# A four-layer graph network on one core: the third layer's factored rows stored a chunk later, the first layer's softmax weights by three VectorE operations and two exponents

## The reference, cut to what matters

```python
x = _layernorm(x + _L0_gnn_ref(x, edge_index, edge_weight, edge_attr_64, ...))
x = _layernorm(x + _L1_gnn_ref(x, src, dst, W1, b1, W2, b2))
x = _layernorm(x + _L2_gnn_ref(x, weight, src, dst, edge_type_8))
x = _layernorm(x + _L3_gnn_ref(x, W_e, b_e, W_n, b_n, src, dst, edge_type_3, node_type_3))

# first layer, per edge and head (alpha is the score)
alpha = jnp.where(alpha >= 0, alpha, 0.2 * alpha)
amax = jax.ops.segment_max(alpha, dst, num_segments=n)
ex = jnp.exp(alpha - amax[dst])
denom = jax.ops.segment_sum(ex, dst, num_segments=n)
attn = ex / (denom[dst] + 1e-16)
out = jax.ops.segment_sum(v[src] * attn[:, :, None], dst, num_segments=n)

# third layer
hw = jnp.einsum('ni,rio->nro', h, weight)     # 8 relations
out = jax.ops.segment_sum(hw[src, rel], dst, num_segments=n_nodes)
```

## Time and profile before

| | |
|---|---|
| median of 3 runs | 1840.75 us (1837.97 to 1842.14) |
| the profiled execution's own time | 1843.65 us |
| its span | 1841.9 us |
| busy: PE, DVE, ACT, POOL | 78%, 77%, 60%, 67% of the span |
| moved by DMA | 205.06 MB, 111 GB/s in the mean |
| mean granted TensorE clock | 0.89 of full speed |

### The profile page before, as it was taken

The page is one execution under the profiler, slowest core; times in us unless marked ns, Lnnn a source line. Parts: engine busy times, 40 slices in busy tenths (PEclk is TensorE's granted clock), DMA queues, the critical chain, the costliest instruction groups (busy, mean ns, idle before and its releaser), DMA issues.

```text
span 1841.9 us, 22899 instructions
## 1 busy us (share of the span) xinstructions
PE 1438.7 (78%) x6078; PEld 924.2 (50%) x6078; DVE 1419.5 (77%) x3056; ACT 1111.6 (60%) x2769; POOL 1237.0 (67%) x910
## 2 busy tenths in 40 slices
PE   4788888888886677777677767766677599999995
PEld 2555555555554566666544444443444355555553
DVE  5798999999998699999876565555665577887874
ACT  1687878787878588888854444444445434434432
POOL 7888887777788777788664444444454258888874
PEclk8788888888888799999898888888788899999998
DMA  6344444444434467676623333333333433433420
GB/s 161 96 101 109 108 106 104 109 105 112 108 94 117 103 164 184 186 186 187 177 75 93 92 92 93 110 104 107 96 82 86 131 88 93 103 92 93 107 77 21
DMA packets 165797, 205.06 MB, mean 111 GB/s; under 512 B 66825, under 2 KB 97920, under 8 KB 165668
## 3 DMA queue, kind: packets, MB, share of 16 engines
q1 hardware_dynamic: 108068, 179.45, 35.3%
q0 software_dynamic: 57600, 24.15, 7.7%
HBM read 147.12 MB, written 70.80 MB: 118 GB/s over the span
## 4 chain that ended last, share of the span: by engine, by line
PE 49%; DVE 19%; ACT 12%; issue 10%; DMA 6%; SPq 3%; POOL 0%; DVEq 0%; ACTq 0%; POOLq 0%
PE po L1369 21%; DMA rel<-in_etype 6%; PE pb L1604 6%; PE pt L1358 6%; DVE bst L755 5%; DVE run L830 3%; PE pc L1478 2%; ACT x L1067 2%; PE po L1364 2%; PE po L1429 2%; ACT so L1263 2%; DVE masked L965 2%; PE pa L1618 2%; PE pa L1645 1%; PE pb L1645 1%
## 5 line engine op out<-in xcount | busy, mean ns | idle before, releaser
L533 POOL DMA_INDIRECT xs<-target_rows,slot_all x236 | 320.6, 1359 | 290.9 <-DMA xs<-source_rows 213.9
L1067 ACT ACTIVATE x<-y,nmr,rst 125x128 f32<-125x128 f32 x800 | 322.5, 483 | 162.5 <-DVE nmr L780 161.7
L1369 PE MATMUL po<-wnt,rt 128*125 128x384 f32 x800 | 297.6, 518 | 0.0
L965 DVE SCALAR_TENSOR_TENSOR masked<-rel,st 128x500 f32<-128x500 int32 x175 | 107.0, 671 | 189.0 <-DMA rel<-in_etype 173.3
L1358 PE MATMUL pt<-ident,x 125*128 125x125 f32 x800 | 133.0, 293 | 112.4 <-issue 112.4
L1369 PEld LDWEIGHTS po<-wnt,rt 128*125 128x125 f32 x800 | 162.8, 206 | 97.3 <-issue 21.8
L1369 PE MATMUL po<-wnt,run 128*125 128x384 f32 x600 | 201.5, 486 | 0.0
L540 POOL DMA_INDIRECT out_rows<-do,last_all x100 | 146.5, 1465 | 65.4 <-issue 44.7
L1358 PEld LDWEIGHTS pt<-ident,x 125*128 125x128 f32 x800 | 102.4, 155 | 149.8 <-issue 148.8
L533 POOL DMA_INDIRECT xs<-in_x,src_all x100 | 146.0, 1460 | 34.6 <-issue 34.3
L1067 ACT ACTIVATE do<-yd,nmr,rst 125x128 f32<-125x128 f32 x400 | 163.7, 483 | 6.2 <-DVE nmr L780 6.2
(11 more groups left out here) (190 smaller groups left out, 3106.5 us busy)
## 6 DMA issues: line engine op xcount, KB each, us to landing
xin<-in_x SPq DMA_DIRECT2D x100, 224.0 KB
out_rows<-res SPq DMA_DIRECT2D x100, 224.0 KB
source_rows<-so SPq DMA_DIRECT2D x75, 224.0 KB
target_rows<-do SPq DMA_DIRECT2D x75, 224.0 KB
xs<-source_rows SPq DMA_DIRECT2D x59, 224.0 KB
same<-same_d SPq DMA_DIRECT2D x50, 250.0 KB
rel<-in_etype SPq DMA_DIRECT2D x50, 250.0 KB
xd<-target_rows SPq DMA_DIRECT2D x46, 224.0 KB
```

The lines of the kernel that those rows point to most:

```text
L533: return nc.gpsimd.indirect_dma_start(out=to, out_offset=None, in_=table, in_offset=bass.IndirectOffsetOnAxis(ap=index, axis=0), bounds_ch ...
L965: V.scalar_tensor_tensor(out=masked[:, r, :], in0=rel[b][:, :], scalar=float(r), in1=st[:, :], op0=ALU.is_equal, op1=ALU.mult).then_inc(q[ ...
L1067: last = A(to[:, j, :], y[:, j, :], ACT.Identity, scale=rst[s][:, k:k + 1], bias=nmr[s][:, k:k + 1])
L1369: last = mm(po[0:R, j * 512:j * 512 + NT * D], left(j), wnt[:, k, :, :].rearrange("k t d -> k (t d)"), start=start, stop=stop, skip_group_ ...
```

## The change

Two things change. In SP's loop of the third layer, `store_sources2(c + 1)` stands where `store_sources2(c + 2)` stood, and ahead of the loop `sources2(3)` is issued before `store_sources2(0)`, while `store_sources2(1)` moves into the loop. In the first layer, the scan adds `aux` first and takes the maximum with the score second, so that `run` holds the running maximum itself; `aux` is no longer shifted. VectorE then makes both exponents' arguments itself (three operations for one), and ScalarE takes two exponents, without the two Relus. A DMA of 4 bytes and a memset at the start fall away.

```diff
@@ SP @@
-            sp.dma_start(row(start_d[0:1, 0:E]), start_p[:, :]).then_inc(s_scr, 16)
-            sp.dma_start(start_d[0:1, E:E + 1], start_p[0:1, 0:1]).then_inc(s_scr, 16)
+            sp.dma_start(row(start_d), start_p[:, :]).then_inc(s_scr, 16)
...
-                sp.dma_start(aux[b][:, :], start_d[0:1, bass.ds(c * C + 1, C)].broadcast_to([D, C])).then_inc(q["aux"][b], 16)
+                sp.dma_start(aux[b][:, :], to_all(start_d, c)).then_inc(q["aux"][b], 16)
...
-            sp.wait_ge(s_scr, 32)
+            sp.wait_ge(s_scr, 16)
...
             stored(1)
+            sources2(3)
             store_sources2(0)
-            sources2(3)
-            store_sources2(1)
...
                 if c >= 1:
                     store2(c - 1)
-                if there(c + 2):
-                    store_sources2(c + 2)
+                if there(c + 1):
+                    store_sources2(c + 1)
                 store_dense(d - 7)
@@ VectorE @@
-            V.memset(run[:, 0, 0:1], -BIG)
...
-                step(scan(run, 0, score, aux[b][:, :], ALU.max, ALU.add))
-                V.tensor_tensor(wb, run[:, 0, 0:C], score, ALU.subtract).then_inc(q["vE"], 1)
+                step(scan(run, 0, aux[b][:, :], score, ALU.add, ALU.max))
+                step(V.tensor_tensor(wb, run[:, 0, 0:C], aux[b][:, :], ALU.add))
+                V.tensor_tensor(wa, score, run[:, 0, 1:C + 1], ALU.subtract)
+                V.tensor_tensor(wb, wb, run[:, 0, 1:C + 1], ALU.subtract).then_inc(q["vE"], 1)
@@ ScalarE @@
-            def differences0(c):
-                q = ph[0]
-                act.wait_ge(q["vE"], c + 1)
-                A(wa, wb, ACT.Relu)
-                A(wb, wb, ACT.Relu, scale=-1.0).then_inc(q["eR"], 1)
-
             def weights0(c):
                 q = ph[0]
-                act.wait_ge(q["eR"], c + 1)
-                A(wb, wb, ACT.Exp, scale=-1.0)
-                A(wa, wa, ACT.Exp, scale=-1.0).then_inc(q["eX"], 1)
+                act.wait_ge(q["vE"], c + 1)
+                A(wb, wb, ACT.Exp)
+                A(wa, wa, ACT.Exp).then_inc(q["eX"], 1)
...
                     evacuate_rt(2 * c)
-                    differences0(c + 1)
                     evacuate_xt(2 * c)
                     weights0(c + 1)
```

More of the change, by code:

```diff
@@ L68, in gnn_kernel @@
     same_d = nc.dram_tensor("same_d", [1, E], F32).ap()
-    start_d = nc.dram_tensor("start_d", [1, E + 1], F32).ap()
+    start_d = nc.dram_tensor("start_d", [1, E], F32).ap()
     rdeg_d = nc.dram_tensor("rdeg_d", [1, E], F32).ap()
@@ L173, in gnn_kernel @@
         SOONER = 13
-        SINGLE = ("tS tD eS eD eL pA pB pR vA vE vL eX eR nS nD nF yb eN sc", "tS tD eS eD pR vA nS nD rd vF",
+        SINGLE = ("tS tD eS eD eL pA pB pR vA vE vL eX nS nD nF yb eN sc", "tS tD eS eD pR vA nS nD rd vF",
                   "tS eS pM pR vA vM nD nF nS", "tS tD eS eD pM pR vM vA eX vN nD rd bs xb")
@@ L1144, in slopes0, with weights0 @@
                 A(score, pc[:, 0:C], ACT.Copy, scale=0.2).then_inc(q["eL"], 1)
-            def differences0(c):
+            def weights0(c):
                 q = ph[0]
                 act.wait_ge(q["vE"], c + 1)
-                A(wa, wb, ACT.Relu)
-                A(wb, wb, ACT.Relu, scale=-1.0).then_inc(q["eR"], 1)
-            def weights0(c):
-                q = ph[0]
-                act.wait_ge(q["eR"], c + 1)
-                A(wb, wb, ACT.Exp, scale=-1.0)
-                A(wa, wa, ACT.Exp, scale=-1.0).then_inc(q["eX"], 1)
+                A(wb, wb, ACT.Exp)
+                A(wa, wa, ACT.Exp).then_inc(q["eX"], 1)
             def sums0(c):
@@ L1178, in _ @@
             slopes0(0)
-            differences0(0)
             weights0(0)
```

## The result

The changed kernel takes 1774.55 us (median of 4 runs, 1769.67 to 1775.76) beside 1840.06 us for the kernel before: a ratio of 0.964, 95% interval [0.962, 0.966], 65.5 us less. The forecast was 1767, the range 1736 to 1796. The profiled executions give 69.0 us between their spans, 1841.9 and 1772.9.

What follows compares the result with a forecast made beforehand. The prediction took a ring of waits through the types' load to bound the third layer: 22 turns of 3.42 us (-75) and +2 for the first layer gave 1770.7 against the profiled 1843.65, so 1767 against the median, range 1736 to 1796.

Steps and rivals of the forecast that it cites:

- The bound and the ring: Third layer: bound by no engine but by a ring of waits through the types' load, one turn 22.39 us.
- Issue time, 2.57 us a turn: Third layer, SP's queue: 2.57 us a turn saved from the end of L1263 to the issue of rel.
- rel's own wait: Third layer: rel's wait for the masks of c+1 is met at 1207.8, over 7 us before L1263 ends.
- The landing, 0.85 us: Third layer: rel lands 4.2 us after issue with 250 KB ahead instead of 1 MB, a gain of 0.85.
- Rival (a): Third layer: only issue time is saved, rel still lands 5.07 us after it; 1786 us, chance 0.15.
- TensorE's part at nothing: Third layer: TensorE's pieces in the ring change with the clock, either sign possible; none taken in the sum.
- (c): Third layer: the clock holds, the ring's eight matmuls take 3.36 us instead of 5.43; 1721 us, chance 0.1.
- (d): Third layer: the slow stretch falls on the matmuls, 6.72 us instead of 5.43; 1795 us, chance 0.1.
- 22 turns alike: Third layer: 3.42 us saved in each of 22 turns, -75 us.
- (e): Third layer: rel comes a whole turn earlier and 173.3 us of waits go; 1669 us, chance 0.02.
- The first layer: First layer: VectorE's added 1.36 us a chunk eats idle time of 1.43; bounds 0 to 34 us, +2 taken.
- rival (f): First layer: slower, 1.36 us on top of each of 25 chunks, +34 us; 1875 with no third-layer gain; chance 0.03.

Runs made afterwards that it cites:

- types_first: The kernel after, with the types' load issued ahead of the sources' load and its wait for ScalarE's factored rows: 1664.54 us, ratio 0.905.
- types_once: The kernel after, with the types' load left out of the third layer's loop (first two chunks' types used for all): 1665.36 us.
- pair_between: The kernel after, with one pair of DMAs (the dense store) put back between the sources' load and the types' load: 1804.60 us, ratio 0.981.
- types_last: The kernel after, with the targets' and same flags' loads issued ahead of the wait for ScalarE's factored rows: 1742.80 us, ratio 0.947.
- weights_only: The kernel before with only the first layer's weights changed, the third layer as before: 1843.04 us, ratio 1.001.
- vector_more: The kernel after, with two more VectorE tensor_tensor of 128x500 in each chunk of the first layer: 1806.82 us, ratio 0.982 to the kernel before.

## Why the prediction was right or wrong, point by point

- **The bound and the ring: right.** The types' load closed the ring; types_first and types_once show that with this load early, or gone, no other ring holds a turn above the engines' own 13.1 us. The turn of 22.39 us that the prediction shows is one of the longer ones; the mean is 21.28.
- **The wait moves, it doesn't go: right.** SP's wait for L1263 moved to the sources' load.
- **Issue time, 2.57 us a turn: right in a full turn, 2.40 in the mean.** From the end of the factored rows to the issue of rel it is mostly 0.86 us for 3.39. In the last three of the 19 turns the kernel before had no dense load in front any more (2.56 us), so there was less to save.
- **rel's own wait: a misreading without effect.** The text before the prediction and the prediction let `relations2(c + 2)` wait for the masks of chunk c+1. The code (L382 of the kernel after) waits for those of chunk c, which used the same buffer and were done a turn earlier.
- **The landing, 0.85 us: mis-sized.** It is 0.30 (5.16 to 4.86, means of 21 and 19 turns). I counted the 750 KB that left the front, and not that the same 750 KB now follow without a stop, where SP stood before. pair_between moves one pair (250 KB) from behind to the front again and costs 0.24 us of landing; types_last takes two loads away from right behind and gains 1.0. Rival (a) had the right reason, that it shares the DMA engines with what follows, and lay nearer in this term. What the bytes in front cost with the same ones behind, no run shows.
- **TensorE's part at nothing: right here.** The engines' part is 12.91 us for 12.97, though the mean clock of 1000 to 1300 us rose from 0.81 to 0.87. Of the rivals on the clock neither came: the relation matmuls on masked copies took 618 ns in the mean for 628, where (c) wanted them at the full clock and (d) slower. (d)'s effect fits pair_between, 649 ns at a mean clock of 0.84, 0.48 us a turn; (c)'s begins in types_last, 599 ns, and is whole in types_first, 582 ns in the same window and a clock of 1.00 up to 1220 us. The groups of 1000 to 1300 us, of before, after, pair_between and types_last (busy us, mean ns):

```profile
L1604 PE MATMUL pb<-masked,wr 128*128 128x500 f32 x190 | 92.3, 628 | 0.0
```

```profile
L1595 PE MATMUL pb<-masked,wr 128*128 128x500 f32 x224 | 106.6, 618 | 0.0
```

```profile
L1597 PE MATMUL pb<-masked,wr 128*128 128x500 f32 x210 | 105.9, 649 | 0.0
```

```profile
L1595 PE MATMUL pb<-masked,wr 128*128 128x500 f32 x249 | 114.2, 599 | 0.0
```

The busy times of 1000 to 1300 us of the kernel before, the kernel after and types_last, with the clock third from the end:

```profile
1000.00:1300.00 300.00, 206.58 (x717) 125.32 (x716) 178.13 (x386) 132.35 (x341) 134.75 (x98) 0.81 0.35 98
```

```profile
1000.00:1300.00 300.00, 238.14 (x832) 144.48 (x832) 207.46 (x454) 156.48 (x402) 157.04 (x113) 0.87 0.40 114
```

```profile
1000.00:1300.00 300.00, 252.94 (x905) 152.79 (x904) 225.08 (x489) 169.76 (x436) 171.36 (x122) 0.90 0.43 118
```

- **22 turns alike: wrong.** 19 turns gave 2.76 us each, and the last two 12.1 us together. I had read the wait of sources2 as always in front of relations2, and gave (e) 0.02; the code's `if there(c + 4)` takes it away in the last turns, where (e) is just what happened. types_first makes it happen in every turn, and its 1664.5 us are near (e)'s 1669. The shortfall of 19 turns (0.66 us each, 12.6 us) and the extra of the last two (5.3 us over 2 x 3.42) cancelled in part. That the forecast came so near, 1767 for 1774.55, is in this part luck.
- **The first layer: right.** weights_only is 1.7 us slower with an interval of -0.4 to +4.2 us, which takes in nothing and the +2 of the forecast. Idle time of 28.7 us became 6.0, and vector_more shows the cliff behind it: rival (f)'s price of 1.4 us a chunk is paid in full by the next operations added.
- **Slower:** nothing of it was seen. From 960 to 1350 us SP was held elsewhere only once, 2.7 us at L400, for a scan, and L1254 never waited for the row store.

## What to carry to other kernels

In a queue that issues DMAs in order, look for the load that closes a ring, and list what stands in front of it up to the last wait: each pair in front cost 0.9 to 1.6 us a turn here, and the wait with the last pair 5.5. Moving a wait behind three pairs of transfers gave 65 us; putting the load in front of that wait, with one swap of two lines, gave another 110. When a wait stands under a condition, follow the condition to the loop's end: the turns without it show for free what its removal brings. Idle time of an engine is a budget: it took 1.36 us a chunk at no cost that could be measured, and the next 1.4 us a chunk cost 32 us in all.

## What the runs showed of the hardware that I had not expected

A load's time to landing depended on what was issued behind it as well as on what was in front: 5.15 us with 1 MB in front and 750 KB behind, 4.86 with 250 KB in front and 1.5 MB behind, and 3.86 with 250 KB in front and only stores in the 3.3 us behind. Moving 750 KB from the front of the load to behind it gave 0.29 us of landing; taking 500 KB of loads away from right behind it gave 1.0.

The mean clock of TensorE over a stretch did not tell what the matmuls in the ring got. It was 0.81, 0.87, 0.84 and 0.90 in the kernel before, the kernel after, pair_between and types_last, and the engines' part of a turn was 12.97, 12.91, 13.39 and 12.46 us. Only with the gaps gone, in types_first, did the clock stay at its upper level, at 1.00 from 1000 to 1220 us.
